# Gathered rows in the last experts; rotary attention with its maxima among q's rows

## The reference

```python
q = q * cos - jnp.roll(q, 1, axis=-1) * sin      # k alike
scores = jnp.einsum('bhqd,bhkd->bhqk', q, k) / math.sqrt(hd)
attn = jax.nn.softmax(scores, axis=-1)
ctx = jnp.einsum('bhqk,bhkd->bhqd', attn, v)
```

```python
pv, pp = lax.top_k(prio, capacity)
tok = jnp.where(valid, pp // K, 0)
xin = x_flat[tok]
h = jax.nn.gelu(jnp.einsum('ecd,edh->ech', xin, w1) + b1[:, None, :], approximate=False)
out_e = jnp.einsum('ech,eho->eco', h, w2) + b2[:, None, :]
```

## Time and profile before

| | |
|---|---|
| median of 3 runs | 2843.49 us (2841.66 to 2847.01) |
| the profiled execution | 2844.36 us, span 2842.4 us |
| TensorE matmul busy | 2173.5 us, 76% |
| VectorE busy | 1797.3 us, 63% |
| ScalarE busy | 1292.6 us, 45% |
| GpSimd busy | 1193.5 us, 42% |
| mean granted TensorE clock | 0.875 of full speed |

### The profile page before, as it was taken

The page is one execution under the profiler, slowest core; times in us unless marked ns, Lnnn a source line. Parts: engine busy times, 40 slices in busy tenths (PEclk is TensorE's granted clock), DMA queues, the critical chain, the costliest instruction groups (busy, mean ns, idle before and its releaser), DMA issues. The chain is left out here.

```text
span 2842.4 us, 46464 instructions
## 1 busy us (share of the span) xinstructions
PE 2173.5 (76%) x15040; PEld 1506.1 (53%) x15040; DVE 1797.3 (63%) x4896; ACT 1292.6 (45%) x2803; POOL 1193.5 (42%) x1166
## 2 busy tenths in 40 slices
PE   1799999999998678339389996959999999841290
PEld 0466666566667567227245554845555666530180
DVE  3677777776875757301367773748889888943023
ACT  1445454545443237213235553736666666430143
POOL 1424242333421100545422121557777777704453
PEclk9899999999999659569679996979999999955595
DMA  6500000000002000112233331000000000000123
GB/s 202 141 1 0 0 0 0 0 0 0 0 1 67 0 0 1 38 52 73 77 101 84 83 104 53 0 1 1 0 0 0 0 0 0 0 0 29 50 63 96
DMA packets 105972, 93.81 MB, mean 33 GB/s; under 512 B 12380, under 2 KB 92406, under 8 KB 105718
## 3 DMA queue, kind: packets, MB, share of 16 engines
q1 hardware_dynamic: 98198, 76.85, 9.7%
q0 software_dynamic: 7680, 15.81, 1.7%
HBM read 62.15 MB, written 46.26 MB: 38 GB/s over the span
## 5 line engine op out<-in xcount | busy, mean ns | idle before, releaser
L3182 POOL TENSOR_SCALAR mb_w<-mb_duT,mb_bT 128x256 f32<-128x256 f32 x512 | 467.9, 932 | 116.7 <-PE bank L3192 85.3
L3117 DVE TENSOR_TENSOR_SCAN mb_hs<-mb_dA,bank 128x512 f32<-128x512 f32 x256 | 300.8, 1205 | 34.6 <-issue 25.0
L38 POOL TENSOR_TENSOR scrap<-ones 128x1 f32<-128x1 f32 x64 | 12.5, 195 | 694.1 <-DVE gla_ss L420 486.8
L3211 PE MATMUL bank<-mb_hc,ident 128*128 128x512 f32 x512 | 256.1, 624 | 15.7 <-DVE mb_hc L3127 15.4
L3173 ACT ACTIVATE mb_dA<-mb_delta,mb_A 128x255 f32<-128x255 f32 x512 | 216.4, 495 | 8.4 <-DVE mb_hs L3117 8.2
L2339 DVE TENSOR_REDUCE ra_mx<-bank 128x2 f32<-128x512 f32 x256 | 163.6, 686 | 57.4 <-PE bank L2193 54.9
L2429 ACT ACTIVATE ra_pT<-bank 128x512 f32<-128x512 f32 x256 | 141.1, 600 | 114.1 <-PE bank L2215 113.8
L1924 ACT ACTIVATE e_hid<-bank,e_b 128x512 f32<-128x512 f32 (+1 forms) x128 | 81.2, 634 | 214.2 <-PE bank L1965 211.3
L3192 PE MATMUL bank<-ident,mb_w 128*128 128x128 f32 x1024 | 150.0, 280 | 34.3 <-DVE mb_hs L3117 26.3
L1885 POOL DMA_INDIRECT results<-e_y,e_x x112 | 109.1, 974 | 144.1 <-DVE e_y L2000 119.1
L1957 PE MATMUL bank<-ident,e_x 128*128 128x128 f32 x112 | 18.8, 292 | 189.2 <-DMA e_x<-queue 189.2
(11 more groups left out here) (529 smaller groups left out, 6160.3 us busy)
## 6 DMA issues: line engine op xcount, KB each, us to landing
results<-const_empty SPq DMA_DIRECT2D x2, 4096.0 KB
e_got<-results SPq DMA_DIRECT2D x32, 256.0 KB, 3.4
rope_rows<-ra_part SPq DMA_DIRECT2D x48, 128.0 KB, 1.9
ra_k<-rope_rows SPq DMA_DIRECT2D x32, 192.0 KB, 3.3
ra_q<-rope_rows SPq DMA_DIRECT2D x32, 192.0 KB, 4.1
queue<-const_spare_rows SPq DMA_DIRECT2D x1, 4128.0 KB
e_x<-queue SPq DMA_DIRECT2D x8, 516.0 KB, 4.3
e_w<-in_L_ffn_w SPq DMA_DIRECT2D x2, 2048.0 KB, 8.1
```

The lines of the kernel that those rows point to most:

```text
L3117: dve.tensor_tensor_scan(hs[n // 2 % 2][:, n % 2, :, :].rearrange("p c t -> p (c t)"), dA[n % RD][:, :, :].rearrange("p c t -> p (c t)"), ...
L3182: ins = pool.tensor_scalar(w[n % RH][:, h, :], duT[k][:, h, :], bT[k][:, h, n:n + 1], None, ALU.mult)
L3211: ins = pe.matmul(YB[:, :], g.ident[:, :], hc[grp % 2][:, j, :, :].rearrange("p c t -> p (c t)"), start=(n == 0), stop=(n == NS - 1))
```

## The change

The diff, cut to its core. It has three parts.

1. The last router no longer sends rows. SyncE writes the normalised rows to `rows3` in DRAM as they come. From the slots VectorE builds 0/1 matrices of their low seven bits (`is_low`) and of the rest (`is_high`), and 64 matmuls turn them into a table with one entry for each slot: which tile and which row of it has this slot. From it come `g.source` (the token to read) and `g.target` (the result row to write; unused slots get spare rows).
2. In the last experts GpSimd gathers each unit's three tiles by `g.source`, six units ahead, in turn with the scatters, and four input buffers are used.
3. In rotary attention the negated maxima are no longer added by a matmul of their own. ScalarE writes them to DRAM and reads them back as three more rows of q (two DMAs), against rows of ones in k; the contraction is over 51 rows in place of 48. The maxima run two steps further ahead (`LEAD` 2), the offsets are made in step 5, and queries and rotation in step 6. q and k are read back in two halves of four head pairs with a semaphore each.

```diff
+            dve.wait_ge(slots_ready, 2)
+            every = places[:, :, :].rearrange("p k t -> p (k t)")
+            dve.tensor_scalar(parts2[:, 0, :], every, 7, None, ALU.logical_shift_right)
+            step(dve.tensor_scalar(parts2[:, 1, :], every, P - 1, None, ALU.bitwise_and))
+            dve.tensor_copy(high[:, :], parts2[:, 0, :])
+            step(dve.tensor_copy(low[:, :], parts2[:, 1, :]))
+            for q in range(4):
+                if q % 2 == 0:
+                    at = slice(q * ROWS, (q + 2) * ROWS)
+                    dve.tensor_tensor(is_high[:, at, :], g.iota[:, 0:SLOTS].unsqueeze(1).broadcast_to([P, 2 * ROWS, SLOTS]),
+                                      high[:, at].unsqueeze(2).broadcast_to([P, 2 * ROWS, SLOTS]), ALU.is_equal)\
+                        .then_inc(high_ready, 1)
+                at = slice(q * ROWS, (q + 1) * ROWS)
+                dve.tensor_tensor(is_low[q][:, :, :], g.iota[:, :].unsqueeze(1).broadcast_to([P, ROWS, P]),
+                                  low[:, at].unsqueeze(2).broadcast_to([P, ROWS, P]), ALU.is_equal).then_inc(low_ready, 1)
+                dve.wait_ge(high_ready, q // 2 + 1)
+                dve.tensor_tensor(named[:, at, 0, :], is_high[:, at, :],
+                                  g.iota[:, q * ROWS + 1:(q + 1) * ROWS + 1].unsqueeze(2).broadcast_to([P, ROWS, SLOTS]),
+                                  ALU.mult).then_inc(tile_named, 1)
+            own = g.ids[:, :, :].rearrange("p k t -> p (k t)")[:, 0:SLOTS]
+            dve.tensor_scalar(trash[:, :], own, float(RESULTS + P), None, ALU.add)
+            dve.wait_ge(table_psum, 1)
+            step(dve.tensor_scalar(named_as[:, :], cnt_bank[:, 0:SLOTS], float(P), -float(P), ALU.mult, ALU.add))
+            step(dve.tensor_tensor(named_as[:, :], named_as[:, :], cnt_bank[:, SLOTS:2 * SLOTS], ALU.add))
+            dve.scalar_tensor_tensor(out=empty[:, :], in0=named_as[:, :], scalar=-0.5, in1=trash[:, :],
+                                     op0=ALU.is_lt, op1=ALU.mult)
+            step(dve.tensor_scalar(token[:, :], named_as[:, :], TOKENS - 0.5, -float(TOKENS), ALU.is_ge, ALU.mult))
+            dve.tensor_tensor(empty[:, :], empty[:, :], named_as[:, :], ALU.add)
+            step(dve.tensor_tensor(token[:, :], token[:, :], named_as[:, :], ALU.add))
+            step(dve.tensor_scalar(token[:, :], token[:, :], 0.0, None, ALU.max))
+            dve.tensor_copy(g.source[:, :], token[:, :])
+            step(dve.tensor_copy(g.target[:, :], empty[:, :]))
+
+        if by_weight:
+            @block.sync
+            def _(sp):
+                for q in range(4):
+                    sp.wait_ge(kept0, 4 * q + 4)
+                    sp.dma_start(g.rows3[q * 8 * P:(q + 1) * 8 * P, :].rearrange("(t p) c -> p t c", p=P),
+                                 rows[0].rearrange("p (t c) -> p t c", c=ROW)[:, q * 8:q * 8 + 8, 0:P])\
+                        .then_inc(kept_rows, 16)
+                sp.wait_ge(kept_rows, 64)
...
+            if by_weight:
+                return
             pool.wait_ge(kept0, NSEQ)
...
+                    act.wait_ge(high_ready, q + 1)
+                    at = slice(q * 2 * ROWS, (q + 1) * 2 * ROWS)
+                    act.activation(named[:, at, 1, :], is_high[:, at, :], ACT.Copy, scale=g.ids[:, 0, 0:1])\
+                        .then_inc(row_named, 1)
+                return
...
+                pe.wait_ge(low_ready, q + 1)
+                pe.wait_ge(tile_named, q + 1)
+                pe.wait_ge(row_named, q // 2 + 1)
+                for r in range(ROWS):
+                    at = q * ROWS + r
+                    ins = pe.matmul(cnt_bank[:, 0:2 * SLOTS], is_low[q][:, r, :],
+                                    named[:, at, :, :].rearrange("p a s -> p (a s)"), start=(at == 0),
+                                    stop=(at == 4 * ROWS - 1))
+            ins.then_inc(table_psum, 1)
...
-    XR, YR = 3, 4
+    XR, YR = (4, 4) if last else (3, 4)
...
+            def gather(u):
+                e, half = u // 2, u % 2
+                if e >= XR:
+                    pool.wait_ge(t_psum, u - 2 * XR + 1)
+                for t in range(half * HT, (half + 1) * HT):
+                    at = e * TILES + t
+                    pool.indirect_dma_start(
+                        out=x[e % XR][:, t, 0:P], out_offset=None, in_=g.rows3[:, :],
+                        in_offset=bass.IndirectOffsetOnAxis(ap=g.source[:, at:at + 1], axis=0))\
+                        .then_inc(half_loaded[half][e % XR], 16)
+
+            AHEAD = 6
+            if last:
+                for u in range(AHEAD):
+                    gather(u)
             for u in range(N):
                 e, half = u // 2, u % 2
                 pool.wait_ge(y_ready, u + 1)
                 for t in range(HT):
-                    pool.indirect_dma_start(
-                        out=results[:, :], in_=y[u % YR][:, t, :], in_offset=None,
-                        out_offset=bass.IndirectOffsetOnAxis(
-                            ap=x[e % XR][:, half * HT + t, P:ROW].bitcast(U32), axis=0)).then_inc(sent[u % YR], 16)
+                    at = e * TILES + half * HT + t
+                    to = g.target[:, at:at + 1] if last else x[e % XR][:, half * HT + t, P:ROW].bitcast(U32)
+                    pool.indirect_dma_start(out=results[:, :], in_=y[u % YR][:, t, :], in_offset=None,
+                                            out_offset=bass.IndirectOffsetOnAxis(ap=to, axis=0))\
+                        .then_inc(sent[u % YR], 16)
+                if last and u + AHEAD < N:
+                    gather(u + AHEAD)
...
-                pe.wait_ge(x_loaded[e % XR], 16 * (e // XR + 1))
+                if last:
+                    pe.wait_ge(half_loaded[half][e % XR], 16 * HT * (e // XR + 1))
+                else:
+                    pe.wait_ge(x_loaded[e % XR], 16 * (e // XR + 1))
...
+        if not isinstance(n, int) or n >= 3:
+            pe.wait_ge(neg_ready, n - 1)
+        if isinstance(n, int) and n in (1, 2):
             pe.wait_ge(v_ready, n)
...
+        if p == RP // 2 and a == 0:
+            pe.wait_ge(copied2, n * 64 + 64)
...
-            pe.wait_ge(neg_ready, s + 1)
+            pe.wait_ge(neg_loaded, s * 32 + 32)
         if p or not first(s):
             pe.wait_ge(p_ready, s * RH + (2 * p + a - 1))
-        rows, every = slice(64 * a, 64 * a + KR), slice(64 * a, 64 * a + 64)
+        rows = slice(64 * a, 64 * a + MR)
         for t in range(2):
-            out = SB[a][:, t * 256:(t + 1) * 256]
-            pe.matmul(out, kk[k][rows, p, t * P:(t + 1) * P], qz[k][rows, p, :], start=True, stop=False)
-            ins = pe.matmul(out, max_of[every, p:p + 1].broadcast_to([64, P]), neg[k][every, :],
-                            start=False, stop=True)
+            ins = pe.matmul(SB[a][:, t * 256:(t + 1) * 256], kk[k][rows, p, t * P:(t + 1) * P], qz[k][rows, p, :],
+                            start=True, stop=True)
         ins.then_inc(s_psum, 1)
 
     def pe_context(pe, s, k, m):
@@ -2249,7 +2349,7 @@
                             start=True, stop=True)
         ins.then_inc(o_psum, 1)
...
-    OFFSETS = 7
+    OFFSETS = 5
...
-    LEAD = 0
+    LEAD = 2
...
-                if step == 7:
+                if step == 6:
                     pe.wait_ge(x_ready, s)
+            if farther and step == 6:
+                pe_tokens(pe, s + 3)
             if step in (2, 4, 6):
                 pe_context(pe, s, k, step // 2 - 1)
+            if farther and step == 6:
+                pe_queries(pe, s + 3)
             if near and step == OFFSETS:
                 if farther and OFFSETS > 6:
                     pe.wait_ge(xT_ready, s + 4)
                 pe_offsets(pe, s + 1)
-            if farther and step == 6:
-                pe_tokens(pe, s + 3)
-            if farther and step == 7:
-                pe_queries(pe, s + 3)
 
     def pe_end(pe):
         pe_context(pe, NSEQ - 1, (NSEQ - 1) % 3, 3)
@@ -2316,7 +2416,7 @@
     def dve_constants(dve):
         for k in R:
...
+            dve.memset(kk[k][:, :, :], 1.0)
...
-            if step == 7 and farther:
+            if step == 6 and farther:
...
-        act.activation(neg[k][:, :], PR[0][:, 256:512], ACT.Copy).then_inc(neg_ready, 1)
+        if not first(n):
+            act.wait_ge(neg_written, n * 16)
+        act.activation(neg[:, :], PR[0][:, 256:512], ACT.Copy).then_inc(neg_ready, 1)
+        act.wait_ge(neg_ready, n + 1)
+        if not first(n):
+            act.wait_ge(neg_loaded, n * 32)
+        act.dma_start(g.max_dram, neg[:, :]).then_inc(neg_written, 16)
+
+    def act_spread(act, n, k):
+        act.wait_ge(neg_written, n * 16 + 16)
+        if not first(n):
+            act.wait_ge(copied, n * 64 + 64)
+            act.wait_ge(copied2, n * 64 + 64)
+        for a in range(2):
+            act.dma_start(qz[k][64 * a + KR:64 * a + MR, :, :],
```

(32 more changed lines are left out.)

37 lines of the change are left out of this document (26 added, 11 removed).

## The result

The changed kernel took 2868.91 us (median of six runs, 2862.11 to 2878.53) against 2843.62 for the kernel before: 1.0087 times as long, 95% interval 1.0070 to 1.0104. Forecast were 2803 us and a gain. The profiled execution took 2868.27 us, span 2866.5, mean granted clock 0.862 (0.875 before).

The account below looks back on a forecast made before the run. It took VectorE, with TensorE in steps 0 to 2, to pace rotary attention, and GpSimd's sends, then TensorE, the last layer. 2844.4-43.9+0.5 (program start)-2.6+5.8=2804.2; less 0.9, 2803 us; range 2774 to 2822.

Parts of the forecast that it names:

- Steady rotary attention: Rotary attention, 13 steady sequences: -0.2 us each, -2.6 us in sum, as the earlier wait eats most of the saving.
- its ends: First and last sequences of rotary attention: memsets, DRAM trips and dropped work together add 5.8 us.
- memsets: Rotary attention's start: three memsets of k at 1.07 us each, 2.1 if element by element; +2.7 less the cast.
- the last experts: Last router and experts: with gathers GpSimd ends at 2737.2 us against 2781.1, a gain of 43.9 us.
- TensorE's start in the last layer: Last experts: TensorE starts at 2620.4 us, after three gathers and a landing.
- GpSimd's pace: Last experts: gathers at 1.265 us each like scatters; GpSimd needs 122.9 us in all and never idles.
- Rivals B and D: Last layer: B, gathers at 1.6 us each, 2819 us, 0.10; D, table or gather ahead starts late, 2823 us, 0.08.
- the starving of GpSimd by VectorE's copies: Last experts: 16 VectorE copies could lock out GpSimd's DMAs, up to 8.8 us more (2812); left out of the sum.
- the additions that it did count: Last experts, units 0 to 7: VectorE's bias adds lengthen eight scatters by 0.19 us each.
- Rival A: Rotary attention follows TensorE's columns: 16.5 us a sequence, -25 in place of -2.6, 2781 us; chance 0.22.
- Rival C: Rotary attention: granted clock falls to 1.2 GHz, +9 us a sequence, 2875 us with eight sequences; chance 0.05.
- The bare trip at sequence 0: Start of rotary attention: the maxima go out to DRAM and back, adding 5.1 us.

Follow-up runs that it names:

- e15: The changed kernel with plain SyncE reads in place of the 48 gathers, so experts get wrong tokens: 2820.1 us, ratio 0.9917 to the kernel before.
- e11: The kernel before with rotary attention's new order, its second score matmul left out and nothing through DRAM: 2868.0 us, ratio 1.0102.
- e17: The changed kernel run a third time, nothing altered: 2854.4 us, ratio 1.0032 to the kernel before.
- e1: The kernel before with only the new router and last experts (table, gathers), rotary attention as before: 2806.1 us, ratio 0.9873.
- e5: The kernel before without rotary attention's second score matmul, in the old order: 2835.5 us, ratio 0.9966.
- e6: The kernel before with the new rotary attention alone, last experts' weight loads held until the last maxima return from DRAM: 2881.6 us, ratio 1.0125.

## Why the prediction was wrong

Three steps failed. Steady rotary attention was added up at full clock (-2.6), and the clock did not stay; its ends were put at +5.8, without the collision and with memsets at half their price; and the last experts (-43.9) left out that TensorE can stand between its own matmuls. The direction turned on the first two: without the gaps the kernel is still no faster.

**Right.** TensorE's start in the last layer and GpSimd's pace. With the gathers alone, the first gather came 115.9 us after the router's first VectorE instruction, as forecast (2614.3 against 2498.4), by two errors that cancel: in the changed kernel's trace the table took 19.8 in place of 17.8 (`is_high` is 1536 wide, 1.76, where 0.95 was counted), the boundary 3.5 in place of 5.4. A gather with its gap took 1.25 for 1.265. GpSimd then needed 125.3 for 122.9, and waited for TensorE's results for 0.9 of it. TensorE waited for gathers from the ninth unit on, where the forecast had "about unit 11". Rivals B and D did not come. Nor did the starving of GpSimd by VectorE's copies that the prediction weighed and left out; the additions that it did count cost twice what it gave them. Rival A (0.22) did not come either: no period was near 16.5, and the columns that go gave 0.9 us a sequence of 3.5 even in the old order.

**A tail of +4.6 that was not seen.** With the gathers alone the span ends 10.3 us after the last store is issued, against 5.8 before. The experts have nine more semaphores, which GpSimd clears one by one at a block's end, but that is not it: the kernel with plain reads (e15) has the same semaphores and ends 6.1 us after its last store. The time comes with the gathers on GpSimd; why it lies at the end is open.

**Steady rotary attention: the term -2.6 was +1.6 at full clock, and the step sooner costs.** The working found VectorE's stretch of steps 3 to 0 at 10.9 to 11.15 and for steps 0 to 2 a gain of 0.53 less 0.3. Measured were 11.26 and 7.31, sum 18.57. The old order with the same matmuls needs 11.0 and 6.54, sum 17.55. So the columns that go are worth 0.9 a sequence (0.66 of it in steps 0 to 2), and what comes with the new order costs 1.0, of which e11's 18.3 leaves some 0.7 to the order itself, where 0.3 was counted: with the rotation in step 6 the reduces of steps 7 and 0 come back to back, nothing runs ahead, and VectorE then waits 1.47 us in step 1 (0.63 in the old order).

**Rival C was the mechanism, and had 0.05.** The forecast took the old order's high load as the measure and asked only whether the clock would stay; it did not ask what a fall would look like. C was priced as whole sequences at 1.2 GHz, +9 each, from five on. What came were bursts: half of the periods from the third on were 0.7 to 5.2 us longer, 14 us in all in the profiled execution, and 20 to 25 by the doubled scores. How many there are differs from execution to execution: the same kernel took from 2836 to 2869 us within the runs of e17. No whole period ran at 1.2 GHz: the longest from the third on, at a mean clock of 0.58, took 24.5 us, 5.9 more than at 1.00. The earlier trace rows held the warning: for 11 of 18 us VectorE has no gap, so matmuls removed beside it become rests of TensorE and not time. Its "near 85%" came true (15.8 of 18.56 us); the comparison set against it, the selective scan with 1.00 at 90%, was of no use, as that stage is busier.

**The ends: +5.8 was about +20.** The memsets were at their upper bound, 2.14 each ("2.1 if element by element"). The Trainium skill states this (VectorE: DVE Perf Modes, "Zero memsets can be issued as uint32 (trn2)": "A `memset` takes one cycle per element whatever the dtype"), and the trace agrees: one f32 memset of 768 and one bf16 memset of 2048 take 2.95 us from start to start (1424.14 to 1427.09), 1.05 ns an element, and those of 768 f32 before took 0.77 each, 1.0 ns. By the row that the forecast chose it was half. The bare trip at sequence 0 was right (5.5 for 5.1; its four parts add up to 5.3). The collision at sequence 14 was missing altogether. The loads were there before, with nothing that they could hold up; the change put a DRAM round trip under them. Memsets, trip, collision, clock and steady term are 5.3+5.5+9.7+14+1.6=36 of the 39.4; the rest lies in the first two periods and the last steps, where the granted clock was lower than before (0.84 against 1.00 in the second period).

**Issue gaps.** Nearly all of the last layer's shortfall (-24.9 for -43.9, 19.0) came from them: from the first gather to the last scatter's end GpSimd took 141.8 us with the gaps and 125.3 without, 16.5 more. Without them the stage takes 241.2 us, -41.5 against before (e1). The sum had TensorE at 5.6 us a unit whenever its inputs are there; no row of before shows otherwise, and what brings the gaps stays open.

## What to carry to other kernels

Taking matmuls out of a stage that another engine paces can lower TensorE's granted clock and cost more than it saves: look where the rests lie before and after, and test by adding harmless matmuls back. Moving a small handover from SBUF to DRAM exposes it to the bulk loads that run at that moment (9.7 us here); look for these in time, not only in size. A reorder and a saving should be timed apart: here the saving alone was worth 10 us, and with the reorder it lost 28.

## What the runs showed of the hardware

- The granted clock fell to 1.2 GHz behind rests of at most 0.9 us (waits of TensorE between 1465 and 1735 in the changed kernel), and with the same matmuls in another order it was 0.97 or 0.80 over 200 us. What decides between these two is open. Each score matmul issued twice brought it to 1.00, and the kernel was 12 to 17 us faster with more work.
- TensorE can stand between independent matmuls without a releaser in the profile: in some groups of runs, and there in every kernel with gathers, gaps of up to 1.8 us, 16 to 20 us in a stage of 125. Kernels without gathers, profiled in two of these groups (e5, e6, e11), have none. So something that comes with the new last layer is needed, perhaps GpSimd's denser stream of indirect DMAs; alone it is not enough, as three groups with it had no gaps. Plain reads were not tried in a group with gaps.
- A VectorE addition with two inputs in SBUF made the GpSimd indirect DMA beside it take up to 1.51 us in place of 0.97 (e1; 1.07 to 1.51 in eight of eight). VectorE's copies from PSUM, where they stood alone beside an indirect DMA, did not: 0.94 to 1.00.
